# Attention's lead-in in a four-stage transformer kernel: queries of the first heads stacked in two halves, keys stacked ahead, GpSimd combining tiles 4 to 15 in batches of four gathers

## The chip, the cores and the metric

The kernel runs on one core of a Trainium2 chip, as one launch. The metric is the device time of that launch in microseconds (us), lower is better; the profile shows one execution of it. The engines are called as the profile calls them: PE (TensorE, matmuls), PEld (its weight loads), DVE (VectorE), ACT (ScalarE), POOL (GpSimd) and SP (SyncE). SPq, ACTq and POOLq are the instruction queues of those engines where they only wait or issue transfers.

## What is computed

The reference takes x of shape (4, 512, 512) and a context ctx of shape (4, 512, 128) through four steps, each added to x with a gate: a learned sparse adjacency, a mixture of 8 experts (two per token) with a shared expert, a grouped cross attention, and a feed-forward layer whose inputs are quantized in blocks of 32. The change touches the end of the second step and the beginning of the third:

```python
x = x + tanh(g_ffn[0]) * moe(layernorm(x))        # y = sum of two experts' rows, by weight; plus shared
# third step: q = layernorm(x) (4, 512, 512), k = v = ctx; 32 query heads, 8 key heads, head size 16
qh = q.reshape(B, S, 8, 4, 16).transpose(0, 2, 3, 1, 4)
kh = k.reshape(B, S, 8, 16).transpose(0, 2, 1, 3)
scores = einsum('bkgsd,bktd->bkgst', qh, kh) / 4
out = einsum('bkgst,bktd->bkgsd', softmax(scores), vh)
x = x + tanh(g_xattn[1]) * out
```

## The kernel before

All engine programs are written out by hand, each in its own order; semaphores tie them together, and nothing is reordered by a scheduler. The 2048 tokens are 16 tiles of 128 rows (TT = 16), four tiles to a batch (R = 4, B = 4). A tile of X is 128 x 512 in float32 and stays in SBUF.

The stages run one after the other: a (adjacency), b (experts), c (attention), d (feed-forward). At the end of stage b every token's two expert rows lie in a DRAM scratch. `gather(t)` (L1168) fetches both rows of tile t on POOL's queue with two indirect transfers of 256 KB, into one of four buffers `mgath`. Adding them to X by their weights is called combining here. DVE combines with `combine(t)` (L1726, L1731) and takes the tile's row statistics (L1736, bn_stats); POOL combines with `combine_late(t)`: two scalings (L1473), a sum (L1476) and an add to X (L1478). Before, DVE combines tiles 0 to 6 and POOL tiles 7 to 15 (`FIRST_LATE = 2 * R - 1`), where POOL issues the next tile's two gathers after each tile.

Attention works on groups: one group is one key head with its four query heads (G = 8 groups to a batch, HG = 4 heads). For each group PE first computes all scores once, with queries as rows, in eight slots (tp, h) of two 128 x 512 matmuls (L1629, `a_slot`), and DVE takes the row maxima of each slot from PSUM (L1798, `max_slot`). The maxima are transposed and laid into a row of QS, and PE computes the scores again with keys as rows (L1641, `b_slot`), ACT takes the exponentials (L1547) and PE multiplies them with V (L1652, `pv`). Maxima run two groups ahead: while group g goes through exponentials, the slots of group g + 2 are mixed in, and a slot's matmul waits until DVE is through with the slot two before it.

QS and KK hold queries and keys split into a high and a low float16 part and stacked in three terms, so each group needs three transfers of 64 KB for queries (`stack_queries`, or L1391 in `stack_group`) and three of 32 KB for keys. Before batch 0 there is a lead-in with the following steps: gathers of tiles 0 to 3; their combining and statistics on DVE; `moments(0, R)`, 4 aggregations and 12 small linked operations (L170 to L176) that give mean and reciprocal deviation; `norm(0, r)` (L1772); transposes on PE (L1604, `t_q`); the high part copied by ACT (L1520, `hi_q`), the low part by DVE (L1779, `lo_q`); the stacking of groups 0 and 1; 16 slots of scores and maxima for groups 0 and 1; then batch 0, group 0. ACT issues the keys of groups 0 and 1 (L1579), SP the queries (L1385). SP waits for the low part of the last row tile before it issues any:

```python
sp.wait_ge(t_free, tuse(None, "q", R - 1) + 1)
for g in range(2):
    stack_queries(0, g)
```

In DVE's batch 0, `combine_stats(t)` at places listed in STATS_AT takes the statistics of tiles that POOL combined (it waits on `mg_used`), and `moments_part` does the moments of tiles 4 to 7 in eight pieces during group 0 (L184 to L193: a seed of three operations, then squares and steps), which `norm(1, r)` needs from group 1 on. `values(0, h)` (L1465) fills V on POOL, eight small scalings behind two fills (L1456, L1460).

## Time and profile before

| | us |
|---|---|
| median of three runs | 1646.1 |
| lowest and highest run | 1642.47, 1647.3 |
| the profiled execution's own time | 1643.61 |
| its span, first to last instruction | 1641.7 |
| PE busy in the span | 1463.1 (89%) |
| DVE busy | 1208.8 (74%) |
| ACT busy | 745.2 (45%) |
| POOL busy | 555.6 (34%) |

Times in the rows are microseconds from the start of the span. The lead-in lies between the last expert matmul, which starts at 639.67, and batch 0 of attention at about 695; attention ends at about 1091. In rows of the timeline a group of equal instructions in a row is one line with its count, and its second number is from the first start to the last end. A matmul's duration holds its pipeline, so in a row of matmuls the distance between starts is what each costs. PEclk is the granted clock of TensorE: 1.00 is 2.4 GHz and 0.50 is 1.2 GHz.

### The profile page before, as it was taken

Reading aid. Unit: us, or ns where it says so; the run is one execution under the profiler, and the core shown is the slowest. Engines: PE = TensorE matmul, PEld = TensorE weight load, DVE = VectorE, ACT = ScalarE, POOL = GpSimd, SP = SyncE. Lnnn points to the kernel's source line nnn. Section 1 sums busy time; section 2 is a strip of 40 time slices with the busy share of each in tenths; the row PEclk is TensorE's granted clock in tenths of the full one; section 3 lists DMA queues with packets and bytes.
Section 4 is the critical chain, followed back from the end, with each engine's and each line's share of the span. In section 5 each row is a group of like instructions: output and inputs, shape, how many; then the busy total and the mean of one; then the engine's idle time right before and its main releaser. Section 6 shows DMA issues by size and latency. Waiting matters only on the chain.

```text
span 1641.7 us, 24188 instructions
## 1 busy us (share of the span) xinstructions
PE 1463.1 (89%) x8146; PEld 708.7 (43%) x8146; DVE 1208.8 (74%) x2087; ACT 745.2 (45%) x1346; POOL 555.6 (34%) x530
## 2 busy tenths in 40 slices
PE   3288898958999996599999999988999999999998
PEld 1145555635555563133232333324444454444444
DVE  6988889466999995999997988855555455555565
ACT  3664654224555555077777777761222222222212
POOL 2523334013676664871010000012323222322332
PEclk8589998988999998599999999999999999999999
DMA  4312222124556554672203011362000000000000
GB/s 158 106 52 68 67 73 86 48 78 152 191 179 191 183 181 130 159 141 48 44 2 59 7 27 32 52 114 41 1 0 26 0 0 15 11 0 0 26 13 13
DMA packets 114811, 113.79 MB, mean 69 GB/s; under 512 B 59416, under 2 KB 87320, under 8 KB 114720
## 3 DMA queue, kind: packets, MB, share of 16 engines
q1 hardware_dynamic: 106448, 89.64, 20.4%
q0 software_dynamic: 5680, 18.62, 4.1%
q10 hardware_dynamic: 2592, 4.39, 0.7%
q8 instruction: 49, 0.80, 0.2%
q14 instruction: 42, 0.34, 0.1%
HBM read 59.26 MB, written 31.20 MB: 55 GB/s over the span
## 4 chain that ended last, share of the span: by engine, by line
PE 61%; DVE 19%; POOL 6%; issue 6%; ACT 4%; DMA 3%; SPq 1%; DVEq 0%; POOLq 0%; ACTq 0%
PE PS L2213 18%; PE PS L2236 10%; PE PS L1039 7%; PE PS L1652 6%; PE PS L1641 6%; PE PS L1629 5%; PE PS L1054 3%; DVE WORK L1798 3%; POOL WORK L2054 2%; PE PS L2226 2%; POOL WORK L2061 1%; DMA WORK<-in_L_ffn_sw_dram 1%; DVE WORK L691 1%; ACT BIG L1547 1%; PE PS L1617 1%
## 5 line engine op out<-in xcount | busy, mean ns | idle before, releaser
L2213 PE MATMUL PS<-BIG 128*128 128x512 f16 x1536 | 337.9, 380 | 3.5 <-issue 2.1
L1798 DVE TENSOR_REDUCE WORK<-PS 128x2 f32<-128x1024 f32 x256 | 302.6, 1217 | 40.9 <-PE PS L1629 39.8
L1547 ACT ACTIVATE BIG<-PS 128x512 f32<-128x512 f32 x512 | 278.7, 596 | 91.6 <-PE PS L1641 86.2
L2213 PEld LDWEIGHTS PS<-BIG 128*128 128x128 f16 x1536 | 150.5, 98 | 182.2 <-issue 3.8
L1629 PE MATMUL PS<-BIG 128*128 128x512 f16 x512 | 189.5, 397 | 14.4 <-DMA BIG<-BIG 7.0
L1641 PE MATMUL PS<-BIG 128*128 128x512 f16 x512 | 193.6, 385 | 3.7 <-ACT BIG L1547 2.0
L1039 PE MATMUL PS<-BIG,WORK 128*128 (+1 forms) x1128 | 180.7, 318 | 14.8 <-DVE WORK L1074 8.0
L2236 PE MATMUL PS<-BIG 128*128 128x512 f16 x768 | 173.8, 379 | 1.8 <-DVE BIG L2308 1.8
L2139 ACT ACTIVATE WORK<-PS 128x512 f32<-128x512 f32 x64 | 38.1, 597 | 296.5 <-PE PS L2213 296.5
L2288 DVE SCALAR_TENSOR_TENSOR BIG<-PS,WORK 128x512 f32<-128x512 f32 x64 | 44.1, 690 | 136.9 <-ACT WORK L2139 136.8
L1039 PEld LDWEIGHTS PS<-BIG,WORK 128*128 128x128 f16 x1128 | 109.8, 99 | 79.2 <-issue 21.4
L1652 PE MATMUL PS<-BIG 128*32 128x512 f32 x1024 | 136.2, 604 | 0.6 <-ACT BIG L1547 0.6
L285 POOL TENSOR_TENSOR BIG<-WORK,BIG 128x704 f16<-128x704 f32 (+2 forms) x49 | 70.9, 1455 | 169.6 <-ACT BIG L269 169.5
L2004 POOL TENSOR_TENSOR BIG<-BIG,WORK 128x2048 f32<-128x2048 f32 (+1 forms) x19 | 59.9, 3153 | 194.5 <-DVE WORK L1993 194.5
L1641 PEld LDWEIGHTS PS<-BIG 128*128 128x128 f16 x512 | 48.9, 97 | 171.7 <-ACT BIG L1547 133.9
L2236 PEld LDWEIGHTS PS<-BIG 128*128 128x128 f16 x768 | 75.1, 98 | 81.8 <-DVE BIG L2308 2.0
L1054 PE MATMUL PS<-BIG,WORK 128*128 (+1 forms) x423 | 99.9, 382 | 5.6 <-DVE WORK L1083 4.7
L1039 PE MATMUL PS<-BIG 128*128 128x352 f16 x576 | 93.6, 321 | 1.5 <-DVE BIG L1074 1.5
L2008 POOL TENSOR_TENSOR BIG<-BIG,WORK 128x2048 f32<-128x2048 f32 (+1 forms) x19 | 59.2, 3115 | 66.8 <-DVE BIG L2000 66.8
L1629 PEld LDWEIGHTS PS<-BIG 128*128 128x128 f16 x512 | 49.7, 99 | 63.9 <-DVE WORK L1798 25.1
L2143 ACT ACTIVATE BIG<-PS 128x512 f16<-128x512 f32 x64 | 36.6, 596 | 84.4 <-PE PS L2226 84.4
L1465 POOL TENSOR_SCALAR BIG<-WORK,GATES 128x64 f32<-128x64 f32 x32 | 15.9, 502 | 172.1 <-PE PS L1652 171.9
(257 smaller groups left out, 2269.4 us busy)
## 6 DMA issues: line engine op xcount, KB each, us to landing
wdq_scratch<-WORK SPq DMA_DIRECT2D x48, 256.0 KB, 2.3
WORK<-in_L_ffn_w_dram SPq DMA_DIRECT2D x32, 352.0 KB, 3.5
y_scratch<-WORK SPq DMA_DIRECT2D x39, 256.0 KB, 2.1
BIG<-BIG SPq DMA_DIRECT2D x96, 64.0 KB, 2.3
X<-in_x_dram SPq DMA_DIRECT2D x4, 1024.0 KB, 9.0
WORK<-in_L_ffn_w_dram SPq DMA_DIRECT2D x16, 256.0 KB, 2.7
WORK<-in_L_ffn_gate_w_dram SPq DMA_DIRECT2D x16, 256.0 KB, 3.2
WORK<-in_L_ffn_up_w_dram SPq DMA_DIRECT2D x16, 256.0 KB, 3.3
```

What stands on the lines that cost most here:

```text
L285: nc.gpsimd.tensor_tensor(chunk_dst(j, slot, 1), chunk_stage(j), chunk_dst(j, slot, 0), ALU.subtract).then_inc(split_l, 1)
L1039: ins = nc.tensor.matmul(bank[1 + 2 * w13 + pair][:, 0:I], m.xT[:, p, a, k * P:(k + 1) * P], W13[:, bass.ds(slot * W13N + (w * half + k * ...
L1054: ins = nc.tensor.matmul(dst[:, :], m.hT[:, up, a, k * P:(k + 1) * P], W2[:, bass.ds(slot * W2N + (w * (W2N // 2) + k * D), D)], start=(fi ...
L1547: nc.scalar.activation(PB[:, tp, 2 * h + j, :], src, ACT.Exp, scale=SOFT_SCALE).then_inc(exp_ok, 1)
L1629: ins = nc.tensor.matmul(APAIR[h % 2][:, i, :], QS[:, g * HG + h, r * P:(r + 1) * P], KA[:, g, :], start=True, stop=True)
L1641: nc.tensor.matmul(BBANK_END[(2 * h + j) % 4] if end else BBANK[j], KS[:, g, t * P:(t + 1) * P], QS[:, g * HG + h, :], start=True, stop=Tr ...
L1652: ins = nc.tensor.matmul(OBANK[32 * h:32 * h + 32, :], V[:, t, g, :], PB[:, tp, 2 * h + j, :], start=(t == 0), stop=(t == R - 1))
L1798: v.tensor_reduce(MXU[:, g % 2, c:c + 2], APAIR[h % 2], AX_X, ALU.max, negate=True).then_inc(max_ok, 1)
L2004: nc.gpsimd.tensor_tensor(blocks(x), blocks(x), spread(sc[:, 1, :], nb), ALU.mult).then_inc(s.q_ok, 1)
L2008: nc.gpsimd.tensor_tensor(blocks(x), blocks(x), spread(sc[:, 2, :], nb), ALU.mult).then_inc(s.dq_ok, 1)
L2213: ins = nc.tensor.matmul(bank[b], fxT[:, p, a, k * P:(k + 1) * P], w[:, c, l, k, :], start=(i == 0), stop=(i == 3 * KD - 1))
L2236: ins = nc.tensor.matmul(dst, fhT[:, a, k, :], DW[:, k // KD, l, k % KD, :], start=(k == 0 and i == 0), stop=(k == FT - 1 and i == 2))
```

## The change

Five things change; what is computed and the instructions' shapes stay as they are, except that three query transfers become six.

- SP issues the queries of group 0 in two halves: the columns of row tiles 0 and 1 as soon as the low part of row tile 1 is there, the rest after row tile 3 with a semaphore of its own (`q_rest`), on which PE waits before the slots of tp = 1.
- ACT issues the keys of groups 0 and 1 before its copies `hi_q`, and DVE takes the keys' low part (`lo_ctx`) behind tile 0's combining instead of behind the moments.
- `FIRST_LATE = R`: DVE combines tiles 0 to 3 only, POOL tiles 4 to 15.
- POOL first fills KK's rows and V and runs `values(0, h)`, then works in three rounds: eight transfers that gather four tiles, then four tiles combined. Outputs of heads (`heads_in`) move to fit.
- The statistics of tiles 4 to 7 are taken by DVE in the first four slots of group 0 of batch 0, the pieces of their moments two to a slot in the last four slots; tiles 8 to 15 have theirs in groups 2 to 5 instead of 1 to 4.

```diff
@@ -1003,7 +1003,7 @@
         mg_in = [sem(f"mg_in{p}") for p in range(len(mgath))]
         mg_half = sem("mg_half")
         mg_used = sem("mg_used")
-        FIRST_LATE = 2 * R - 1
+        FIRST_LATE = R
 
         class Unit:
 
@@ -1334,6 +1334,7 @@
         t_hi = sem("t_hi")
         t_free = sem("t_free")
         qk_in = [sem(f"qk_in{g}") for g in range(G)]
+        q_rest = sem("q_rest")
         a_mm = sem("a_mm")
         max_ok = sem("max_ok")
         mt_ok = sem("mt_ok")
@@ -1379,10 +1380,11 @@
             def load_ctx(b):
                 sp.dma_start(CT, ctx_rows[:, bass.ds(b * R, R), :]).then_inc(ct_in, 16)
 
-            def stack_queries(b, g):
+            def stack_queries(g, cols, landed):
                 for n, (a, w) in enumerate(TERMS):
                     rows = slice(n * HD, (n + 1) * HD)
-                    sp.dma_start(QS[rows, g * HG:(g + 1) * HG, :], qhT[g * HD:(g + 1) * HD, a, :, :]).then_inc(qk_in[g], 16)
+                    sp.dma_start(QS[rows, g * HG:(g + 1) * HG, cols],
+                                 qhT[g * HD:(g + 1) * HD, a, :, cols]).then_inc(landed, 16)
 
             def stack_group(b, g):
 
@@ -1431,9 +1433,11 @@
             load_ctx(0)
             sp.wait_ge(pad_low, 1)
             sp.wait_ge(pad_high, 1)
+            sp.wait_ge(t_free, tuse(None, "q", 1) + 1)
+            stack_queries(0, slice(0, 2 * P), qk_in[0])
             sp.wait_ge(t_free, tuse(None, "q", R - 1) + 1)
-            for g in range(2):
-                stack_queries(0, g)
+            stack_queries(0, slice(2 * P, S), q_rest)
+            stack_queries(1, slice(0, S), qk_in[1])
             for g in range(2, 4):
                 stack_group(0, g)
             maxima(0, 0, 0)
@@ -1454,11 +1458,9 @@
         def c_gpsimd(pool):
             g = nc.gpsimd
             nc.gpsimd.memset(KK.rearrange("p a b c -> p (a b c)")[32:64, :].bitcast(F32), 0.0).then_inc(pad_low, 1)
-            for t in range(len(mgath), 2 * len(mgath)):
-                gather(pool, t)
             pool.wait_ge(pad_low, 1)
-            nc.gpsimd.memset(V.rearrange("p a b c -> p (a b c)"), 1.0).then_inc(v_ones, 1)
-            pool.wait_ge(v_ones, 1)
+            nc.gpsimd.memset(V.rearrange("p a b c -> p (a b c)"), 1.0).then_inc(pad_low, 1)
+            pool.wait_ge(pad_low, 2)
 
             def values(b, h):
                 nc.gpsimd.nop(nofuse=True)
@@ -1488,17 +1490,19 @@
             pool.wait_ge(ct_in, 16)
             for h in range(G):
                 values(0, h)
-            for t in range(R, TT - R):
-                if t >= FIRST_LATE:
+            for q in range(1, B):
+                for t in range(q * R, q * R + R):
+                    gather(pool, t)
+                if q == B - 1:
+                    heads_in(0, 1)
+                for t in range(q * R, q * R + R):
                     combine_late(t)
-                gather(pool, t + len(mgath))
+                if q == B - 2:
+                    heads_in(0, 0)
+            pool.wait_ge(ct_in, 32)
             for h in range(G):
-                if h < R:
-                    combine_late(TT - R + h)
-                if h > 0:
+                if h > 2:
                     heads_in(0, h - 1)
-                if h == 0:
-                    pool.wait_ge(ct_in, 32)
                 pool.wait_ge(pv_mm, (h + 1) * 2)
                 values(1, h)
             with pool.Fori(1, B - 1) as b:
@@ -1569,8 +1573,6 @@
             nc.scalar.nop().then_inc(exp_ok, 2)
             nc.scalar.nop().then_inc(o_sb, 1)
             hi_ctx(None)
-            for r in range(R):
-                hi_q(None, r)
             act.wait_ge(pad_low, 1)
             act.wait_ge(t_free, tuse(None, "q", 0))
             for g in range(2):
@@ -1578,6 +1580,8 @@
                     rows = slice(n * HD, (n + 1) * HD)
                     nc.scalar.dma_start(KK[rows, g, :, :], khT[g * HD:(g + 1) * HD, w, :].unsqueeze(1).to_broadcast([HD, 2, S])
                                         ).then_inc(qk_in[g], 16)
+            for r in range(R):
+                hi_q(None, r)
             maxima(None, -1, 0)
             batch(0, True, False)
             with act.Fori(1, B - 1) as b:
@@ -1705,6 +1709,8 @@
                 t_q(None, 0, r)
             for u in range(2):
                 for tp in range(2):
+                    if u == 0 and tp == 1:
+                        pe.wait_ge(q_rest, 16 * 3)
                     for h in range(HG):
                         a_slot(u, u, tp, h, lambda: pe.wait_ge(qk_in[u], 16 * 6), u > 0)
                 if u == 0:
@@ -1762,9 +1768,6 @@
                 else:
                     rsqrt_parts(link, MV[:, a:b, 1], RSTD[:, a:b], b - a)[i - 1]()
 
-            for t in range(R):
-                combine(t)
-            moments(0, R)
 
             def norm(b, r):
                 t = b * R + r
@@ -1838,9 +1841,10 @@
                             if ahead:
                                 max_slot(u + 2, g, tp, h)
                             if first and (g, tp, h) in STATS_AT:
-                                combine_stats(2 * R + STATS_AT.index((g, tp, h)))
-                            if first and g == 0:
-                                moments_part(R, 2 * R, tp * HG + h)
+                                combine_stats(R + STATS_AT.index((g, tp, h)))
+                            if first and g == 0 and tp == 1:
+                                moments_part(R, 2 * R, 2 * h)
+                                moments_part(R, 2 * R, 2 * h + 1)
                             if first and g == G - 1:
                                 moments_part(2 * R, TT, tp * HG + h)
                             if tp == 0 and h == 1 and not last and 1 <= g <= R:
@@ -1876,29 +1880,28 @@
                     rows_aggr(b)
                     rows_end(b)
 
+            combine(0)
+            lo_ctx(None)
+            for t in range(1, R):
+                combine(t)
+            moments(0, R)
             for r in range(2):
                 norm(0, r)
-            lo_ctx(None)
             for r in range(R):
                 if r < 2:
                     dve.wait_ge(t_mm, tuse(None, "q", r) + 1)
                     norm(0, r + 2)
                 lo_q(None, r)
-            for t in range(R, 2 * R - 1):
-                combine(t)
             for u in range(2):
                 for tp in range(2):
                     for h in range(HG):
                         max_slot(u, u, tp, h)
-                        if (u, tp, h) == (1, 1, 0):
-                            combine_stats(FIRST_LATE)
-            STATS_AT = [(g, *at) for g in range(1, 5) for at in ((0, 3), (1, 3))]
+            STATS_AT = [(0, 0, h) for h in range(R)] + [(g, *at) for g in range(2, 6) for at in ((0, 3), (1, 3))]
             batch(0, True, False)
             with dve.Fori(1, B - 1) as b:
                 batch(b, False, False)
             batch(B - 1, False, True)
 
-        v_ones = sem("v_ones")
         oo_ok = sem("oo_ok")
```

How the change moves the instructions, at three places. First DVE from the end of the lead-in's low parts through group 0 of batch 0, before (L1779 is the low part, L1726, L1731 and L1736 combine a tile and take its statistics, L1798 is a slot's maxima, L1747 and L184 to L193 are pieces of the moments):

```order
L1779 TENSOR_TENSOR BIG<-PS,BIG 128x4x128 x3
L1726 SCALAR_TENSOR_TENSOR X<-WORK,X 128x512
L1731 SCALAR_TENSOR_TENSOR X<-WORK,X 128x512
L1736 BN_STATS WORK<-X 128x6
...
L1798 TENSOR_REDUCE WORK<-PS 128x2 x13
L1736 BN_STATS WORK<-X 128x6
L1798 TENSOR_REDUCE WORK<-PS 128x2 x4
L1747 BN_AGGR MV<-WORK 128x2 x4
L1798 TENSOR_REDUCE WORK<-PS 128x2
L184 TENSOR_SCALAR NEWT<-MV 128x4
```

The same place after the change (lines are shifted by 3 to 6):

```order
L1782 TENSOR_TENSOR BIG<-PS,BIG 128x4x128 x3
L1801 TENSOR_REDUCE WORK<-PS 128x2 x17
L1742 BN_STATS WORK<-X 128x6
L1801 TENSOR_REDUCE WORK<-PS 128x2
L1742 BN_STATS WORK<-X 128x6
...
L1801 TENSOR_REDUCE WORK<-PS 128x2
L1753 BN_AGGR MV<-WORK 128x2 x4
L184 TENSOR_SCALAR NEWT<-MV 128x4
L185 TENSOR_SCALAR RSTD<-NEWT 128x4
L186 TENSOR_SCALAR NEWT<-NEWT 128x4
```

The three combined tiles ahead of the first maxima and the one set of statistics among the lead-in's 16 slots are gone; four sets of statistics stand behind the first four slots of group 0.

Second, POOL from the gathers of the lead-in on, before (L1168 is one gather transfer, L1456 and L1460 are the fills, L1465 the values, L1473 to L1478 combine a tile):

```order
L1168 DMA WORK<-y_scratch,WORK 128x512 x8
L1456 MEMSET BIG 32x4096
L1168 DMA WORK<-y_scratch,WORK 128x512 x8
L1460 MEMSET BIG 128x1024
L1465 TENSOR_SCALAR BIG<-WORK,GATES 128x4x16 x8
L1168 DMA WORK<-y_scratch,WORK 128x512 x6
L1473 TENSOR_SCALAR WORK<-WORK 128x512 x2
L1476 TENSOR_TENSOR WORK<-WORK 128x512
L1478 TENSOR_TENSOR X<-WORK,X 128x512
L1168 DMA WORK<-y_scratch,WORK 128x512 x2
```

and after:

```order
L1168 DMA WORK<-y_scratch,WORK 128x512 x8
L1460 MEMSET BIG 32x4096
L1462 MEMSET BIG 128x1024
L1467 TENSOR_SCALAR BIG<-WORK,GATES 128x4x16 x8
L1168 DMA WORK<-y_scratch,WORK 128x512 x8
L1475 TENSOR_SCALAR WORK<-WORK 128x512 x2
L1478 TENSOR_TENSOR WORK<-WORK 128x512
L1480 TENSOR_TENSOR X<-WORK,X 128x512
L1475 TENSOR_SCALAR WORK<-WORK 128x512 x2
```

The second eight gathers moved behind the fills and the values, and combining runs tile after tile with no gathers between.

Third, SP's queue at the stacking, before (L1380 loads the context, L1385 are queries of groups 0 and 1, L1391 and L1392 queries and keys of the groups after):

```order
L1380 DMA WORK<-in_ctx_dram 128x4x128
L1385 DMA BIG<-BIG 16x2048 x6
L1391 DMA BIG<-BIG 16x2048
L1392 DMA BIG<-BIG 16x2x512
L1391 DMA BIG<-BIG 16x2048
```

and after:

```order
L1381 DMA WORK<-in_ctx_dram 128x4x128
L1386 DMA BIG<-BIG 16x4x256 x6
L1386 DMA BIG<-BIG 16x2048 x3
L1393 DMA BIG<-BIG 16x2048
L1394 DMA BIG<-BIG 16x2x512
```

Group 0's three query transfers are six of half the size, of which three can go earlier; everything behind them on the queue follows three issues later.

## Rows read from the trace of the kernel before

**Rows 1.** The page, chain that ended last: shares of the span by engine.

```profile
PE 61%; DVE 19%; POOL 6%; issue 6%; ACT 4%; DMA 3%; SPq 1%; DVEq 0%; POOLq 0%; ACTq 0%
```

**Rows 2.** Windows: stretch, length, busy by PE, PEld, DVE, ACT, POOL, then PEclk, DMA, GB/s.

```profile
675.00:695.00 20.00, 15.79 (x33) 2.67 (x34) 18.45 (x18) 0.27 (x1) 17.08 (x19) 0.50 0.65 162
700.00:712.00 12.00, 9.84 (x55) 3.10 (x57) 11.59 (x21) 8.51 (x17) 10.52 (x12) 1.00 0.88 191
712.00:724.00 12.00, 12.00 (x74) 4.11 (x73) 11.81 (x15) 9.54 (x20) 11.01 (x12) 1.00 0.80 163
```

**Rows 3.** Chain in order of time: start, length, what, from the lead-in to group 0.

```profile
663.93 1.13 PE PS L1604 x4
...
668.70 0.70 DVE BIG L1779
...
669.49 0.64 SPq L1385
...
670.80 4.20 DMA BIG<-BIG
675.04 1.05 PE PS L1629 x2
676.11 9.43 DVE WORK L1798 x8
```

**Rows 4.** Timeline of DVE: start, length, line, operation, shapes, count, idle before.

```profile
666.77 1.39 DVE L1779 TENSOR_TENSOR BIG<-PS,BIG 128x512 f16<-128x512 f32 x2
...
672.25 0.75 DVE L1731 SCALAR_TENSOR_TENSOR X<-WORK,X 128x512 f32<-128x512 f32 x1
...
692.71 0.68 DVE L1736 BATCH_NORM_STATS2 WORK<-X 128x6 f32<-128x512 f32 x1
693.31 3.56 DVE L1798 TENSOR_REDUCE WORK<-PS 128x2 f32<-128x1024 f32 x3
697.35 1.23 DVE L1798 TENSOR_REDUCE WORK<-PS 128x2 f32<-128x1024 f32 x1 [0.48 <-PE PS L1629]
...
700.04 0.79 DVE L184 TENSOR_SCALAR NEWT<-MV 128x4 f32<-128x4 f32 x1
700.86 0.17 DVE L185 TENSOR_SCALAR RSTD<-NEWT 128x4 int32<-128x4 int32 x1
...
705.34 0.82 DVE L189 TENSOR_TENSOR NEWT<-RSTD 128x4 f32<-128x4 f32 x1
...
711.48 1.21 DVE L1798 TENSOR_REDUCE WORK<-PS 128x2 f32<-128x1024 f32 x1
```

**Rows 5.** Timeline of POOL, and ACT's one row of key transfers.

```profile
655.61 3.50 POOL L1456 MEMSET BIG<- 32x4096 f32 x1
...
670.71 5.22 POOL L1465 TENSOR_SCALAR BIG<-WORK,GATES 128x64 f32<-128x64 f32 x8 [0.21 <-POOL BIG L1460]
676.08 1.01 POOL L1168 DMA_INDIRECT WORK<-y_scratch,WORK  x1
...
683.40 1.36 POOL L1473 TENSOR_SCALAR WORK<-WORK 128x512 f32<-128x512 f32 x2
...
687.72 1.04 POOL L1168 DMA_INDIRECT WORK<-y_scratch,WORK  x1 [0.27 <-POOL X L1478]
...
699.53 1.27 POOL L1478 TENSOR_TENSOR X<-WORK,X 128x512 f32<-128x512 f32 x1
...
668.13 4.35 ACTq L1579 DMA_DIRECT2D BIG<-BIG  x6
```

**Rows 6.** Transfers issued in 694.5 to 698.5, then in 776 to 782: size, us to landing.

```profile
BIG<-BIG SPq DMA_DIRECT2D x4, 32.0 KB, 3.5
...
BIG<-BIG SPq DMA_DIRECT2D x5, 32.0 KB, 2.0
```

**Rows 7.** Windows as in Rows 2, in stage a, where the granted clock fell.

```profile
276.00:280.00 4.00, 1.90 (x27) 1.55 (x26) 3.97 (x4) 1.61 (x3) 4.00 (x3) 0.97 0.00 0
280.00:283.00 3.00, 3.00 (x11) 1.57 (x10) 2.82 (x7) 0.00 (x0) 2.76 (x3) 0.50 0.00 0
```

## The prediction

> **What bounds the kernel now.** I read the chain that ended last first: PE holds 61% of it and DVE 19% [rows 1]. That is an average, so the windows around the edit come next [rows 2]. From 675 to 695, the lead-in's 16 slots, DVE is busy 18.45 of 20.00 us and ACT 0.27: nothing goes through exponentials yet, and PE runs at a granted clock of 0.50, its lower level of 1.2 GHz. From 700 to 712, group 0 of batch 0, the clock is at 1.00, DVE is busy 11.59 of 12.00 and PE 9.84. From 712 on PE is busy 12.00 of 12.00 with DVE close behind at 11.81. So DVE sets the pace up to the end of group 0, and PE after it. A gain in the lead-in counts only if DVE does not lose it again in group 0.
>
> The chain in order of time gives the lead-in's path [rows 3]: the last low part ends at 669.40 (668.70 + 0.70), SP's first query issue starts at 669.49, the third transfer runs from 670.80 to 675.00, PE starts its slots at 675.04 and DVE its maxima at 676.11. Between 669.3 and 675.9 DVE combines tiles 4 to 6, in time that it would otherwise spend waiting for that transfer.
>
> **The lead: first queries earlier.** SP waits for row tile 1 instead of row tile 3. Two low parts in a row started at 666.77 and ended together at 668.16 [rows 4]; the first is row tile 1, so it ends about 0.69 after 666.77, at 667.46. With SP's lag from before (669.40 to 669.49) the first issue starts at 667.56, and the third, 1.31 behind it as 670.80 is behind 669.49 [rows 3], at 668.87. How long half a transfer takes beside a running gather has no row; the ends are 2.0 (32 KB with no gather) and 4.20 (64 KB among keys, queries and gathers), and the nearest is 3.5, 32 KB with gathers running [rows 3, 6]. I take 3.5, because in the changed order POOL's second eight gathers are in flight just then. Landing at 672.4 instead of 675.0: **2.6 earlier**, between 1.9 and 4.1.
>
> Edits that must hold for this and cost nothing: the keys. ACT can issue them once KK's fill is done at 659.11 [rows 5], and six issues took 4.35, so it is through at 663.5, while its first copy waits for transposes that end at 665.06 (663.93 + 1.13) [rows 3]. If that cover of 1.6 were gone, the difference would move the whole path. The keys' low part on DVE behind tile 0 is 0.69 of work at a place where DVE waits for gathers (tile 3's data come last either way). The second half of the queries is issued after 669.40 and behind three issues, so its third lands about where group 0's did before, at 675.0 or a little earlier; PE needs it after four slots, which take DVE 4.7 of the 9.43 for eight [rows 3], so at about 677. It is hidden by 2. What is queued behind it on SP (queries of group 1, then 12 issues and the maxima's row) has less lateness than the slots of groups 0 and 1 give it, 19 us from 676.11 to the end.
>
> Taking tiles 4 to 6 from DVE saves nothing by itself: they filled a wait. It has to be done, since their 6.6 us would now stand in front of the maxima. The statistics of tile 7 did stand among the slots, at 692.71, and the next slot started at 693.31 [rows 4]. **0.6 earlier.**
>
> **What comes back in group 0.** DVE takes the statistics of tiles 4 to 7 behind the first four slots of group 0, four times 0.60: **2.4 later**. Before, group 0 took DVE from 697.35 to 711.48, 14.13 without an idle row but for the 0.48 ahead of it [rows 4], so nothing there hides them, at either clock. The pieces of the moments are the same operations, only two to a slot. What they wait for on POOL may change. At 700.04 the first seed took 0.79, and its neighbour 0.17; POOL's add to X ran from 699.53 to 700.80 [rows 4, 5]. The 0.82 at 705.34 holds the same kind of excess, so the two largest make 0.62 + 0.65 = 1.3. DVE's small operations wait out a large POOL operation there.
>
> After the change POOL gets to its first round at about 665 (fill, V's fill, then eight values of 5.22 or less [rows 5]). Six gathers took 7.32, from 676.08 to 683.40; eight take about 9.8. A tile takes 4.05 (683.40 to 687.45, where POOL is free for the gather at 687.72 after 0.27). Tiles 4 to 7 are done at about 665 + 9.8 + 16.2 = 691, and DVE asks for the first at about 695: **no wait**. The second round gathers until about 701 and then combines without a pause up to 717. The moments' pieces come at about 702 to 709, so they meet POOL at work all the time, where before it was at work 4.05 of every 6.68. On the other side they stand in four bundles behind four slots rather than in seven. The bounds: all 1.3 gone, or each of four bundles waiting out two POOL operations of about 1.0 each (4.05 for four), 8 in all, 6.7 more. I take the value of before, **0 more**, as nearest row, with both ends kept.
>
> **POOL's values beside DVE's moments.** The eight values now run beside the lead-in's 12 linked operations and `norm`, which lie on the path. Before, they ran beside DVE's combining, and the combining operation at 672.25 took 0.75 as others did without POOL's company [rows 4]; POOL's eight took 5.22, so POOL waited rather than DVE. I take 0; the other end is 3.5, eight times a POOL operation of 0.44 if none could pass. The Trainium skill, SBUF — State Buffer, "Who interferes with whom", says that a DVE instruction with two SBUF inputs and a GpSimd instruction that reads SBUF exclude each other, and that the second to issue is held until the first is through. The 0.79 at 700.04 agrees with that; the 0.75 at 672.25 does not, as far as small POOL operations go. By the rule alone the sum would be up to 3.5 worse.
>
> **The sum.** -2.6 - 0.6 + 2.4 + 0 + 0 = -0.8 us. After group 0 PE is the bound and its work is unchanged; group 1 loses two sets of statistics and group 5 gains them, where DVE has room. The profiled execution took 1643.61, so it would take 1642.8; it lies 2.5 under the median of 1646.1, and I give the forecast against the median: 1645.3.
>
> **Rivals.** *The lead carries through.* The moments' pieces fall between POOL's operations and the half transfers land in 2.0: -4.1 - 0.6 + 2.4 - 1.3 = -3.6, 1642.5. For it: POOL's phase is free by several us. Against: gathers are in flight and combining is unbroken. *POOL holds up the moments.* Each of the four bundles loses 1.0 to 2.0 to POOL's combining: 4.0 to 8.0 instead of 1.3, so -0.8 + 2.7 to 6.7 = +1.9 to +5.9, 1648.0 to 1652.0: slower than before. It decides once the waits in group 0 exceed 1.3 + 0.8 = 2.1. For it: POOL without a pause from 701 to 717. *The values hold up the lead-in.* Up to +3.5, so +2.7, 1648.8; the row at 672.25 speaks against it, the skill's rule for it. *The clock.* In group 0 PE now has four matmuls for each 1.8 of DVE's work (3.56 for three slots, 1.19 each, and 0.60) in the first half. In stage a a stretch in which PE was busy 1.90 of 4.00 was followed by a granted clock of 0.50 [rows 7]; the 9.84 of 12.00 in group 0 before was not [rows 2]. A fall for three or four us makes the second half's matmuls twice as long and costs about 2: 1647.3. *The change does not do what it says*: the halves land after 4.2 beside the gathers, and 1.9 - 2.6 leaves -0.1: 1646.0, which the forecast's range holds.
>
> **How the numbers follow.** Forecast with its range of 1643.5 to 1647: 0.52. Lead carries through: 0.18. POOL holds up the moments: 0.18. Values: 0.05. Clock: 0.07. A measurement of this kernel can tell about 0.3% from no change, 4.9 us here. Faster by more than that needs the first rival with all its terms at their ends: 0.06. Slower by more needs the upper half of POOL's hold or two rivals at once: 0.05. The rest, 0.89, is within. The range of 8 in 10 reaches from 1641.0 to 1649.0: the forecast's terms between their bounds, the lower half of POOL's hold, and the runs' own spread, whose lowest lies 3.6 under their median.
>
> **What would show it.** In the changed profile: PE's first slot at about 672.4 instead of 675.04, with no wait on the second half before the fifth; DVE's maxima back to back from there; DVE's first maximum of group 0 at about 694.2 instead of 697.35, and group 1's first at about 710.7 instead of 711.48, so 3.2 gained and 2.4 lost again. Waits of DVE on POOL's tiles 4 to 7, key issues that end after 665, moments in the lead-in longer than before, or small operations in group 0 beyond 2.1 us of excess would each prove a step wrong. So would a span over 4.9 us shorter, since no term here is that large.

## The result and the profile after

The changed kernel takes 1647.83 us in the median of 20 runs, the kernel before 1644.31 in 20 runs beside them. The ratio is 1.0019, 95% interval 1.0010 to 1.0028: slower by 0.19%, some 3.1 us. One of the 20 runs of the changed kernel took 2214.41 at a mean granted clock of 0.647, against 0.947 to 0.953 in the other 19, and the ratio leaves it out. The change is smaller than the 0.3% that the prediction thought could be told, but the interval lies wholly above 1; the forecast was 0.8 us less. The 1647.83 is outside the forecast's own range (1643.5 to 1647) and inside the wide one (1641.0 to 1649.0). The forecast started from a median of 1646.1 for the kernel before; 3.1 more than that is 1649.2, just above the wide range. The profiled execution has a span of 1647.6.

The chain that ended last has the shares of before [rows 1], with PE at 60% instead of 61% and DMA at 2% instead of 3%:

```profile
PE 60%; DVE 19%; POOL 6%; issue 6%; ACT 4%; DMA 2%; SPq 1%; DVEq 0%; POOLq 0%; ACTq 0%
```

So the windows come next, as in [rows 2]: stretch, length, busy by PE, PEld, DVE, ACT and POOL, then the granted clock, DMA share and GB/s. The three stretches are the lead-in's 16 slots, group 0 of batch 0, and the start of group 1:

```profile
676.00:696.00 20.00, 16.33 (x35) 2.77 (x34) 17.92 (x16) 0.27 (x1) 18.56 (x20) 0.50 0.51 111
700.00:717.00 17.00, 11.13 (x59) 3.25 (x57) 16.55 (x28) 8.91 (x17) 15.79 (x18) 1.00 0.73 167
717.00:724.00 7.00, 5.89 (x37) 2.04 (x36) 6.62 (x7) 4.80 (x10) 1.84 (x2) 1.00 0.10 18
```

Group 0 is where the change shows. PE was busy 9.84 of 12.00 there [rows 2] and is now busy 11.13 of 17.00; DVE is busy nearly throughout, and POOL 15.79 of 17.00.

The lead did come earlier. The chain in order of time, as in [rows 3] (start, length, what), from the low part of row tile 1 to the first maxima:

```profile
669.87 0.61 DVE BIG L1782
...
670.57 0.76 SPq L1386
...
672.01 3.56 DMA BIG<-BIG
...
675.62 1.05 PE PS L1633 x2
676.69 3.59 DVE WORK L1801 x3
```

Its times can't be set beside those of before directly, because this execution reached the end of stage b later: the last row of expert matmuls starts at 642.27, against 639.67. All times in the next table are worked out as the start of a row minus the start of that last expert row in the same trace. "Excess" is what the 12 small operations of the moments in group 0 (L184 to L193) took in all beyond 0.165 us each, which is about what one takes with POOL idle.

| us after the last expert row | before | after |
|---|---|---|
| PE's first slot | 35.38 | 33.35 |
| DVE's first maximum | 36.45 | 34.42 |
| group 0's first maximum | 57.68 | 55.14 |
| group 1's first maximum | 71.82 | 74.61 |
| length of group 0 | 14.13 | 19.47 |
| group 2's first maximum | 84.13 | 86.59 |
| batch 1's first maximum | 159.19 | 162.02 |
| end of the span | 1002.03 | 1005.30 |
| excess of the 12 small operations | 1.59 | 4.60 |

The changed kernel is 2.5 us ahead at the start of group 0 and 2.8 behind at its end. The whole loss arises in group 0, and it is still there at batch 1 (2.8) and at the end (3.3). DVE's timeline there (start, length, line, operation, shapes, count, idle before) shows what group 0 is made of now; [rows 4] are the rows of before:

```profile
663.82 0.20 DVE L170 TENSOR_SCALAR NEWT<-MV 128x4 f32<-128x4 f32 x1
...
676.69 9.48 DVE L1801 TENSOR_REDUCE WORK<-PS 128x2 f32<-128x1024 f32 x8 [4.29 <-PE PS L1633]
687.50 9.42 DVE L1801 TENSOR_REDUCE WORK<-PS 128x2 f32<-128x1024 f32 x8 [1.33 <-PE PS L1633]
697.41 1.23 DVE L1801 TENSOR_REDUCE WORK<-PS 128x2 f32<-128x1024 f32 x1 [0.49 <-PE PS L1633]
698.55 0.69 DVE L1742 BATCH_NORM_STATS2 WORK<-X 128x6 f32<-128x512 f32 x1
...
705.85 1.01 DVE L184 TENSOR_SCALAR NEWT<-MV 128x4 f32<-128x4 f32 x1
706.90 0.63 DVE L185 TENSOR_SCALAR RSTD<-NEWT 128x4 int32<-128x4 int32 x1
707.57 0.63 DVE L186 TENSOR_SCALAR NEWT<-NEWT 128x4 f32<-128x4 f32 x1
708.23 1.23 DVE L1801 TENSOR_REDUCE WORK<-PS 128x2 f32<-128x1024 f32 x1
709.37 0.16 DVE L189 TENSOR_TENSOR NEWT<-RSTD 128x4 f32<-128x4 f32 x1
709.57 0.16 DVE L190 TENSOR_TENSOR NEWT<-NEWT 128x4 f32<-128x4 f32 x1
709.77 1.13 DVE L193 SCALAR_TENSOR_TENSOR RSTD<-NEWT,RSTD 128x4 f32<-128x4 f32 x1
...
712.45 1.12 DVE L193 SCALAR_TENSOR_TENSOR RSTD<-NEWT,RSTD 128x4 f32<-128x4 f32 x1
...
714.95 0.62 DVE L190 TENSOR_TENSOR NEWT<-NEWT 128x4 f32<-128x4 f32 x1
715.60 0.63 DVE L193 SCALAR_TENSOR_TENSOR RSTD<-NEWT,RSTD 128x4 f32<-128x4 f32 x1
```

Beside it POOL's timeline, where [rows 5] stood before:

```profile
663.25 3.35 POOL L1467 TENSOR_SCALAR BIG<-WORK,GATES 128x64 f32<-128x64 f32 x8 [0.21 <-POOL BIG L1462]
...
691.45 1.26 POOL L1480 TENSOR_TENSOR X<-WORK,X 128x512 f32<-128x512 f32 x1
692.87 1.04 POOL L1168 DMA_INDIRECT WORK<-y_scratch,WORK  x1 [0.15 <-POOL X L1480]
...
705.57 1.26 POOL L1480 TENSOR_TENSOR X<-WORK,X 128x512 f32<-128x512 f32 x1
706.82 1.35 POOL L1475 TENSOR_SCALAR WORK<-WORK 128x512 f32<-128x512 f32 x2
708.26 1.26 POOL L1478 TENSOR_TENSOR WORK<-WORK 128x512 f32<-128x512 f32 x1
709.60 1.28 POOL L1480 TENSOR_TENSOR X<-WORK,X 128x512 f32<-128x512 f32 x1
```

The two views are read together by ends. The seed at 705.85 ends at 706.86, POOL's add at 706.83. The next two operations, 0.63 each, end at 707.53 and 708.20, POOL's pair of scalings (706.82, 1.35) at 708.17. The step at 709.77 ends at 710.90, POOL's add at 710.88. Each long small operation ends within 0.03 of the end of a POOL operation; it is called held below. There are 7 of these in group 0, against 3 before: the 0.79 and 0.82 of [rows 4] and this one:

```profile
710.38 0.46 DVE L193 SCALAR_TENSOR_TENSOR RSTD<-NEWT,RSTD 128x4 f32<-128x4 f32 x1
```

The rows also show why unbroken combining costs more than its share of time. Before, the seed was held once, until POOL's add ended at 700.80. POOL then went over to a gather, so the next operation, at 700.86, took 0.17 [rows 4]:

```profile
701.07 1.05 POOL L1168 DMA_INDIRECT WORK<-y_scratch,WORK  x1 [0.27 <-POOL X L1478]
```

Now the end of one POOL operation is the start of the next, so the following small operation is held again. And being held sets DVE's phase. Released at 708.20, DVE runs a maximum and the first operation of a square, which ends at 709.53, just as POOL's next operation does (708.26 + 1.26). One operation of 0.16 slips in, POOL's add starts at 709.60, and the step at 709.77 waits out nearly the whole of it. Then the same happens again (1.12 at 712.45).

### The profile page after: what moved, and what is told of

It reads as the page before. It is cut to its first block, busy times and chain, and to the rows that moved or that the text cites. A ratio compares the mean times of both kernels' runs of the same rounds, so it can differ in the third digit from the quotient of the medians.

```text
span 1647.6 us, 24194 instructions
## 1 busy us (share of the span) xinstructions
PE 1465.8 (89%) x8146; PEld 709.9 (43%) x8146; DVE 1208.3 (73%) x2081; ACT 744.9 (45%) x1346; POOL 565.4 (34%) x542
## 4 chain that ended last, share of the span: by engine, by line
PE 60%; DVE 19%; POOL 6%; issue 6%; ACT 4%; DMA 2%; SPq 1%; DVEq 0%; POOLq 0%; ACTq 0%
PE PS L2216 18%; PE PS L2239 10%; PE PS L1039 7%; PE PS L1656 6%; PE PS L1645 6%; PE PS L1633 5%; PE PS L1054 4%; DVE WORK L1801 3%; POOL WORK L2057 2%; PE PS L2229 2%; POOL WORK L2064 1%; DMA WORK<-in_L_ffn_sw_dram 1%; DVE WORK L691 1%; ACT BIG L1551 1%; PE PS L1621 1%
## 5 line engine op out<-in xcount | busy, mean ns | idle before, releaser
L1487 POOL TENSOR_TENSOR X<-WORK,X 128x256 f32<-128x256 f32 (+1 forms) x32 | 23.2, 726 | 157.1 <-DVE WORK L1812 157.1
```

## The experiments

All ratios are to the kernel before, run on the same chip. The theory is that of the rival in the prediction: POOL's combining holds up the moments' small operations.

**POOL pauses while the moments run.** The changed kernel with one wait in POOL's loop, ahead of the combining of tiles 8 to 11:

```diff
+                if q == B - 2:
+                    pool.wait_ge(qn_ok, R + 1)
                 for t in range(q * R, q * R + R):
                     combine_late(t)
```

> The changed kernel with one wait added: GpSimd gathers tiles 8 to 11 as it did, but combines them only after VectorE has normalized tile 4 for batch 1, so that no combining runs beside the moments' pieces of group 0. Theory 1 (the pieces wait out GpSimd's combining): the excess of the twelve small operations over 0.17 each falls from 4.6 us to under 0.5, group 0 gets 4 to 4.6 us shorter, and the kernel comes out 1.4 us under the kernel before (ratio 0.9991) instead of 3.2 over it. Rival A (VectorE's own work in group 0 is the loss: four sets of statistics, pieces in bundles of two): group 0 keeps its length within 1 us and the ratio stays at about 1.002.

Measured: ratio 0.999, interval 0.9977 to 1.0002. DVE's and POOL's timelines in that kernel:

```profile
704.46 0.17 DVE L184 TENSOR_SCALAR NEWT<-MV 128x4 f32<-128x4 f32 x1
...
706.59 0.16 DVE L193 SCALAR_TENSOR_TENSOR RSTD<-NEWT,RSTD 128x4 f32<-128x4 f32 x1
```

```profile
713.78 1.36 POOL L1475 TENSOR_SCALAR WORK<-WORK 128x512 f32<-128x512 f32 x2 [11.36 <-DVE WORK L1777]
```

With POOL waiting 11.36, the seed takes 0.17 instead of 1.01 and the step 0.16 instead of 1.13. The excess falls from 4.60 to -0.03, group 0 from 19.47 to 14.85: 4.62 less, the whole excess and no more. The ratio falls by 0.0029, 4.8 us, and the two intervals do not overlap. The cause of the loss is shown by this run: the operations, their number and their order on DVE are those of the changed kernel, only POOL is still. Against the kernel before, it is not shown to be faster: the interval reaches over 1.

**Combining and gathers alternate again.** The changed kernel, but POOL issues the gathers of one tile after each combined tile, as before:

```diff
-            for q in range(1, B):
-                for t in range(q * R, q * R + R):
-                    gather(pool, t)
...
-                for t in range(q * R, q * R + R):
-                    combine_late(t)
+            for t in range(R, 2 * R):
+                gather(pool, t)
+            for t in range(R, TT):
+                combine_late(t)
+                if t + R < TT:
+                    gather(pool, t + R)
...
```

> The changed kernel with GpSimd's batches undone from tile 4 on: one tile combined, then the two gathers of the tile four further on, as in the kernel before. Theory 1: GpSimd combines 4.05 of every 6.7 us while the pieces run, so about six tenths of the 4.6 us of waits are left, 2.8; the kernel is 1.4 us over the kernel before (1.0008). Rival A: no change against the changed kernel, 1.002. Rival C (the combining of tiles 4 to 7 then ends too late for the statistics): VectorE waits before the fourth set of statistics, whose tile is combined at about 701, and the time is over 1.002.

Measured: 1.0007, interval 0.9995 to 1.0019. The excess is 2.45 and group 0 takes 17.31, so 2.15 and 2.16 less than in the changed kernel. DVE and POOL:

```profile
702.40 1.17 DVE L185 TENSOR_SCALAR RSTD<-NEWT 128x4 int32<-128x4 int32 x1
703.61 0.17 DVE L186 TENSOR_SCALAR NEWT<-NEWT 128x4 f32<-128x4 f32 x1
```

```profile
702.29 1.27 POOL L1480 TENSOR_TENSOR X<-WORK,X 128x512 f32<-128x512 f32 x1
703.83 1.04 POOL L1168 DMA_INDIRECT WORK<-y_scratch,WORK  x1 [0.27 <-POOL X L1480]
```

A single hold can be as long as ever (1.17, within 0.03 of POOL's end), but the gather behind it lets the next operation through in 0.17. Of the 3.0 by which the excess had grown, 2.15 thus goes with the batching of gathers. The other 0.86 (2.45 against 1.59) may go with the order of the pieces and POOL's phase; no run tells these apart.

**The lead alone.** The kernel before with the half transfers, the earlier keys and the earlier `lo_ctx`; DVE still combines tiles 4 to 6 and POOL's order is that of before:

```diff
...
+            sp.wait_ge(t_free, tuse(None, "q", 1) + 1)
+            stack_queries(0, slice(0, 2 * P), qk_in[0])
             sp.wait_ge(t_free, tuse(None, "q", R - 1) + 1)
-            for g in range(2):
-                stack_queries(0, g)
+            stack_queries(0, slice(2 * P, S), q_rest)
+            stack_queries(1, slice(0, S), qk_in[1])
...
```

> The kernel before with the first part of the change alone: queries of group 0 in two halves, keys stacked ahead of ScalarE's copies, the keys' low part behind tile 0. VectorE still combines tiles 4 to 6 before the first maxima and GpSimd keeps its order. Theory 1: TensorE's first slot starts 2 to 3 us earlier, VectorE's first maximum less than 0.5 us earlier because it is busy combining until then, and the time is that of the kernel before within 0.5 us (ratio 1.000). Rival D (an earlier lead is worth its length whatever VectorE does): 2.6 us faster, 0.9984.

Measured: 1.0003, interval 0.9989 to 1.0017. PE's first slot comes at 33.61, 1.77 earlier than before, DVE's first maximum at 36.32, 0.13 earlier. DVE's timeline says why:

```profile
676.59 0.69 DVE L1742 BATCH_NORM_STATS2 WORK<-X 128x6 f32<-128x512 f32 x1
677.20 9.47 DVE L1800 TENSOR_REDUCE WORK<-PS 128x2 f32<-128x1024 f32 x8
```

The statistics of tile 6 run right up to the maxima, with no idle time between. The three tiles that filled the wait of before now stand in the way, so the earlier transfer is worth nothing unless some of them leave DVE. The excess is 1.87 here, with the pieces and POOL's order of before, so a shift of phase alone moved it by 0.28.

**Whole queries.** The changed kernel with its queries in whole transfers after row tile 3:

```diff
-            sp.wait_ge(t_free, tuse(None, "q", 1) + 1)
-            stack_queries(0, slice(0, 2 * P), qk_in[0])
             sp.wait_ge(t_free, tuse(None, "q", R - 1) + 1)
-            stack_queries(0, slice(2 * P, S), q_rest)
+            stack_queries(0, slice(0, S), qk_in[0])
...
```

> The changed kernel with the halves undone: SyncE waits for row tile 3 and issues whole queries for groups 0 and 1; all else as changed. Theory 1: the lead of 2.0 us (first slot against the last expert matmul) is lost and nothing else changes, so the kernel is 2 us slower than the changed one, 5.2 over the kernel before (1.0032). Rival B (the halves gain nothing because gathers hold them up): same as the changed kernel, 1.002.

Measured: 1.003, interval 1.0016 to 1.0044. PE's first slot comes at 35.61, 2.26 later than in the changed kernel; batch 1 begins 1.55 later (163.57 against 162.02), and the ratio is 0.0011 higher, 1.8 us. The two ratios' intervals overlap, so the times alone do not show it; the trace's 1.55 speaks for the same size. By that pair of traces the halves keep most of what they gain at the first slot, as long as DVE has nothing in front of its maxima. The excess in group 0 is 4.12, near that of the changed kernel, as it should be.

**Short statistics.** The changed kernel with the statistics of tiles 4 to 7 over 32 columns instead of 512:

```diff
-                v.bn_stats(bnst_c[:, t, :], X[:, t, :]).then_inc(row_st, 1)
+                v.bn_stats(bnst_c[:, t, :], X[:, t, 0:32] if R <= t < 2 * R else X[:, t, :]).then_inc(row_st, 1)
```

> The changed kernel with the statistics of tiles 4 to 7 taken over the first 32 columns of a row instead of 512, so the moments of these tiles are those of 32 columns and the output is not the reference's. It prices the term of 2.4 us. If that term is right (four sets of 0.60 each lie open in group 0), the first four slots of group 0 get 4 x 0.5 = 2.0 us shorter (0.69 against about 0.18 for a short one), and group 0 with them, give or take the waits on GpSimd, which change phase. If TensorE at its lower clock hid them, group 0 gets less than 1 us shorter.

Measured: 1.0005, interval 0.9994 to 1.0015; group 0 takes 17.21, 2.26 less, of which 0.29 is a smaller excess (4.31). One statistics operation:

```profile
694.32 0.18 DVE L1742 BATCH_NORM_STATS2 WORK<-X 128x6 f32<-128x32 f32 x1
```

About 0.5 saved four times is what group 0 loses in length: in group 0 of this kernel each microsecond on DVE is a microsecond of the path, for the statistics as for the holds.

**Half operations on POOL.** The changed kernel with POOL's operations on tiles 8 to 11 split into two of 256 columns each:

```diff
+                parts = [slice(0, D // 2), slice(D // 2, D)] if 2 * R <= t < 3 * R else [slice(0, D)]
...
-                g.tensor_tensor(m[:, 0, :], m[:, 0, :], m[:, 1, :], ALU.add).then_inc(mg_half, 1)
+                for n, c in enumerate(parts):
+                    ins = g.tensor_tensor(m[:, 0, c], m[:, 0, c], m[:, 1, c], ALU.add)
+                ins.then_inc(mg_half, 1)
...
```

> The changed kernel, no pause, with GpSimd's operations on tiles 8 to 11 cut into halves of 256 columns. Theory 1 with the length of one GpSimd operation as the price: each wait of a small operation lasts at most 0.75 us (a half sum) instead of 1.13, and the excess of the twelve falls from 4.6 us, to 2.3 if their number stays; since halves follow each other without a semaphore between, more of the twelve may have to wait, so up to 4.6. If a wait lasted for GpSimd's whole row of queued operations, single excesses would stay at 1 us or more.

One execution, 1647.87, too little to rank by time. The trace tells the size of a hold:

```profile
703.37 0.73 DVE L184 TENSOR_SCALAR NEWT<-MV 128x4 f32<-128x4 f32 x1
704.14 0.65 DVE L185 TENSOR_SCALAR RSTD<-NEWT 128x4 int32<-128x4 int32 x1
...
706.82 0.58 DVE L193 SCALAR_TENSOR_TENSOR RSTD<-NEWT,RSTD 128x4 f32<-128x4 f32 x1
```

The longest falls from 1.13 to 0.73, the excess from 4.60 to 3.04. A hold gets shorter with the POOL operation beside it (two half sums now take 1.41); there are 8 holds instead of 7, and the sum falls by a third and not by half.

**Pause, and tile 4 back on DVE.** The changed kernel with the pause, and with one tile combined by DVE in its wait for the queries, which also takes one statistics operation out of group 0:

```diff
-        FIRST_LATE = R
+        FIRST_LATE = R + 1
...
+                if q == B - 2:
+                    pool.wait_ge(qn_ok, R + 1)
-                for t in range(q * R, q * R + R):
+                for t in range(max(q * R, FIRST_LATE), q * R + R):
...
+            for t in range(R, FIRST_LATE):
+                combine(t)
...
```

> The kernel with GpSimd's pause, and tile 4 given back to VectorE, which combines it in its wait for the first scores and takes its statistics there, so that group 0 holds three sets of statistics. Expected by theory 1: the first slot and the first maximum stay where they are, group 0 is 0.6 us shorter than with the pause alone (14.2 instead of 14.85), and the time is 2.0 us under the kernel before (0.9988). Rival: GpSimd's first tile now waits for VectorE's and the statistics of tile 7 come late, so nothing is gained.

Measured: 0.9981, interval 0.9969 to 0.9993: faster than both kernels, 3.1 us under the kernel before. In DVE's timeline the tile fits into the wait with 2.44 left over:

```profile
672.31 0.69 DVE L1746 BATCH_NORM_STATS2 WORK<-X 128x6 f32<-128x512 f32 x1
675.44 9.49 DVE L1805 TENSOR_REDUCE WORK<-PS 128x2 f32<-128x1024 f32 x8 [2.44 <-PE PS L1637]
```

Group 0 takes 14.23 with an excess of -0.04, and batch 1 begins at 157.03, 2.16 earlier than before. That tile 4 on DVE adds anything to the pause is not shown by the times: the intervals overlap (the changed kernel with the pause has 0.9977 to 1.0002), and in that run's trace batch 1 began at 156.77, after a lead-in whose 16 slots ran 1.2 faster, in part at a granted clock of 1.00.

**Pause, and tiles 4 and 5 back on DVE.** The same with `FIRST_LATE = R + 2`.

> As with tile 4, and tile 5 too goes back to VectorE ahead of the first maxima. Its gathers landed at 674.6 in the changed kernel, and a tile takes VectorE 2.2 us with its statistics, so it is done at 676.8 against a first maximum at 676.69. Expected: the first maximum 0 to 0.3 us later, group 0 another 0.6 shorter (13.6), the time 2.3 us under the kernel before (0.9986). Rival: the two tiles hold up the first maxima by more than they save, and the time is that of the version with tile 4 or above.

Measured: 0.9983, interval 0.9971 to 0.9994, not to be told from the last. The wait is now used up; the maxima follow the statistics without a gap:

```profile
675.29 0.69 DVE L1746 BATCH_NORM_STATS2 WORK<-X 128x6 f32<-128x512 f32 x1
675.90 9.47 DVE L1805 TENSOR_REDUCE WORK<-PS 128x2 f32<-128x1024 f32 x8
```

Group 0 takes 13.88, so 0.35 less than with tile 4 alone where 0.6 was expected, and batch 1 begins at 156.84.

**The pause alone, in the kernel before.**

```diff
+                if t == FIRST_LATE + 2:
+                    pool.wait_ge(qn_ok, R + 1)
                 if t >= FIRST_LATE:
                     combine_late(t)
                 gather(pool, t + len(mgath))
+            heads_in(0, 0)
...
```

> The kernel before with the pause alone: POOL waits for the first norm of group 1 before it combines tile 9, so nothing large runs on POOL beside the moments' twelve small operations in group 0 (before: tiles 9 and 10). The output of head 0 moves up two places on POOL to fit. Theory (the small operations lose time to POOL's combining, in the kernel before as well): their excess goes from 1.59 us to about 0, group 0 becomes 1.6 shorter, and the whole is 1.6 us faster, ratio 0.999; the earlier lead and the pause are then separate gains that add up to what the kernel with tile 4 on DVE showed (0.9981, 3.4 us faster). Rival (that kernel's gain is the pause alone): ratio 0.998, no difference to it. Rival (POOL's later tiles and values hold up attention afterwards, which cancels it): 1.000 or above, with group 0 shorter and the time lost in groups 1 to 5.

Measured: 0.9996, interval 0.9986 to 1.0005. The excess goes from 1.59 to -0.08 and group 0 from 14.13 to 12.67, so the kernel before had the same loss in a smaller size. The 1.6 us are seen in group 0; in the time they are not shown, since the interval reaches over 1. In DVE's and POOL's timelines:

```profile
702.69 0.16 DVE L184 TENSOR_SCALAR NEWT<-MV 128x4 f32<-128x4 f32 x1
```

```profile
715.57 1.36 POOL L1473 TENSOR_SCALAR WORK<-WORK 128x512 f32<-128x512 f32 x2 [16.35 <-DVE WORK L1775]
```

Of the 1.44 that group 1 begins earlier, 0.69 is left at batch 1; the rest goes in the groups between, which no run took apart. The rival that the pause alone explains the 0.9981 is not borne out: 0.9981 is outside this interval. It is not excluded either, since the two intervals overlap between 0.9986 and 0.9993. That the gains of the lead and of the pause simply add up is not borne out by the medians (alone they gave 1.0003 and 0.9996), but intervals this wide cannot exclude it. What the runs show is that the lead moves DVE's first maximum by only 0.13 while tiles 4 to 6 stay on DVE, and that tiles on POOL without the pause make the kernel slower.

**All runs together.** In the seven traces where POOL combines beside the moments' pieces 36 small operations are held, and each ends 0.01 to 0.05 after a POOL operation. Group 0 less its excess takes 14.86 to 14.88 in the five runs with the changed kernel's work on DVE (changed, pause, alternating, whole queries, half operations) and 12.54 to 12.74 in the three with the work of before (before, lead alone, before with the pause). So besides the statistics the holds account for the length of group 0 to within 0.2.

## Why the prediction was wrong

Each step, in the prediction's order, with what the changed profile shows. Times are from the table above.

| step | predicted | measured |
|---|---|---|
| lead, first slot of PE | -2.6 (-1.9 to -4.1) | -2.03 |
| tile 7's statistics out of the lead's slots | -0.6 | -0.5 |
| four statistics in group 0 | +2.4 | +2.3 (group 0 less its excess: 14.87 against 12.54); 2.0 of it gone in the run with short ones |
| waits on POOL's combining in group 0 | 0 more (-1.3 to +6.7) | +3.0 |
| values beside the lead-in's moments | 0 (up to +3.5) | 0.1; 0.6 in three later runs |
| group 1's first maximum | -0.8 | +2.8 |

**The step that failed is the term "0 more" for what the moments' pieces wait for on POOL.** It measured 4.60 against 1.59, 3.0 more. The prediction had seen the cause: it names POOL's unbroken combining from 701 to 717 (measured: 702.78 to 718.92) and has a rival for just this, from 1.9 to 5.9 slower, which decides once the waits exceed 2.1. It then took the excess of before as the nearest row and gave the rival 0.18. That row was not near, and it was read at 1.3, the two largest holds, where the 12 operations had 1.59. Before, POOL combined 4.05 of every 6.68, and behind the hold of the seed came a gather, so the next operation took 0.17 [rows 4]. After, there is no gather to slip through, and every bundle has three linked operations. Scaling the excess of before by POOL's busy share alone (6.68 over 4.05, so 1.65 times 1.59) would have given 2.6, already 1.0 more and past the 2.1 from which that rival decides. Of the rest the seed has a large part: its three operations, held one behind the other, have an excess of 1.78 (0.68 before). The run with a still POOL takes the 4.6 away, and the one with alternating gathers takes half of it away. So the forecast falls, and the rival "POOL holds up the moments" is what happened, in the lower half of its range: 4.6 in its four bundles, where it had 4.0 to 8.0.

**The lead** was 0.6 smaller than predicted, still within its bounds. Most of that lies ahead of the transfer: the data of tile 3 land later (DVE combines it from 661.10, 18.83 after the last expert row; before 18.53), so the moments of the lead-in start 21.55 after that row instead of 21.24, and with a slightly slower chain of small operations the low part of row tile 1 ends 0.41 later. SP's third issue comes 1.44 behind its first instead of 1.31. The transfer itself took 3.56, where 3.5 was taken from [rows 6]; the changed kernel's row for these three transfers, as in [rows 6], has a median of

```profile
BIG<-BIG SPq DMA_DIRECT2D x3, 32.0 KB, 3.4
```

so the choice among 2.0, 3.5 and 4.20 was right.

**The covers held.** The keys are issued at 662.06 and through 3.96 later, ahead of ACT's first copy at 668.09:

```profile
662.06 3.96 ACTq L1581 DMA_DIRECT2D BIG<-BIG  x6
```

Their end at 666.02 is past the 665 that the prediction named as a sign of error, but only because this execution runs later as a whole: it is 23.75 after the last expert row, where the predicted 663.5 is 23.83 after the row of before.

PE waited 4.58 for the first half of the queries and nowhere for the second. DVE did not wait for POOL's tiles: tile 7 is combined at 692.71 (691.45 + 1.26), and the first statistics run at 698.55; the prediction said 691 and 695. The eight values on POOL (663.25 to 666.60) ran beside the lead-in's moments, whose 12 operations took 0.16 to 0.20 each, 0.20 for the first one shown above. In the runs with whole queries, with short statistics and with tile 4 on DVE one of them took 0.51, and the 12 had an excess of about 0.6. The value 0 for this term stands within that, and its rival (+3.5) did not happen.

The two sides of the Trainium skill's rule (SBUF — State Buffer, "Who interferes with whom": a DVE instruction that needs the port it shares with GpSimd and a GpSimd instruction exclude each other, and the second to issue is held until the first is through) come apart here. For POOL's operations of 128 x 512 the trace agrees, with holds of up to 1.13 beside operations of 1.27, ending together. For those of 128 x 64 (3.35 for eight, 0.42 each) the same small operations show next to nothing: 0.1 to 0.6 for the 12, where the prediction worked out up to 3.5 by the rule. In the kernel before, where the same eight ran beside DVE's combining, they took 5.22 [rows 5] and DVE's combining 0.73 to 0.77 an operation, about the 0.75 of elsewhere: there POOL was the one that waited. Whether it is the size of the operations that decides was not tried.

**The clock** was no cause. From 700 to 717 the granted clock stayed at 1.00, though PE was busy only 11.13 of 17.00, so the rival that it would fall did not happen. It did fall in group 0 in two other runs, the ones with whole queries and with half operations (windows as above):

```profile
710.80:714.20 3.40, 3.21 (x12) 1.50 (x16) 3.23 (x8) 1.03 (x2) 3.24 (x5) 0.50 0.89 190
```

```profile
706.60:710.00 3.40, 3.40 (x12) 1.45 (x16) 3.24 (x6) 1.28 (x3) 3.26 (x6) 0.50 1.04 222
```

Their group 0 less its excess took 14.86 and 14.87, as in the changed kernel (14.87). So the 2 us that the prediction put on such a fall were not there.

The terms as measured, -2.0 - 0.5 + 2.3 + 3.0, make +2.8, and the trace has +2.8 at group 1. What is behind it adds little: group 1 gets 0.3 back for its two sets of statistics (11.98 instead of 12.31), and batch 1 begins 2.8 behind. The prediction's belief that nothing after group 0 hides or adds much was right for this change. The end of the span is 3.3 behind, near the 3.1 of the ratio, but that closeness is in part luck: ends of single executions vary more, and that of the kernel before with the pause is 2.2 behind the kernel before, at a ratio of 0.9996.

## What to carry to other kernels

Here a chain of 12 short, linked VectorE operations lost 4.60 us beside a GpSimd that combined without a pause, 2.45 where gathers stood between, and nothing beside a still GpSimd. A link of 0.165 could wait for most of a GpSimd operation of 1.27, and the next link for the one after it. So before moving work to GpSimd, look for such chains in the same stretch, count links and not only busy shares, and try keeping GpSimd still while the chain runs (here with one wait). An earlier transfer counted only once the engine that uses its data had less filler work in front of it. How much filler to leave there is open: of the two versions faster than the kernel before, one left 2.44 of the wait unused and the other nothing, and they cannot be told apart.

## What the runs showed of the hardware

Not only the operations with two SBUF inputs were held. The seed, L184 to L186, are operations with one tile as input and constants, and took 1.01, 0.63 and 0.63. The prediction was wrong to read the 0.79 of before, also L184, as a case of the rule on two SBUF inputs. The statistics (0.69 at 698.55, and 0.69 at 703.72 with POOL combining) and the maxima from PSUM (1.21 to 1.23 throughout) were not. The Trainium skill (SBUF — State Buffer, "Who interferes with whom") names `tensor_scalar` among the operations that can take the shared port, if their operands meet its conditions, and says that `tensor_reduce` never does on trn2; these rows agree with both. Which property of an operation decides was not tried.

The granted clock rose once in the lead-in of the changed kernel, and fell again. Windows of that kernel:

```profile
667.00:671.00 4.00, 3.89 (x16) 2.94 (x16) 3.15 (x6) 1.79 (x3) 3.08 (x4) 0.50 0.44 125
671.00:674.40 3.40, 0.04 (x1) 0.00 (x0) 0.86 (x2) 0.60 (x1) 2.48 (x4) 1.00 0.83 213
674.40:698.00 23.60, 18.71 (x39) 3.49 (x40) 19.43 (x17) 1.46 (x3) 21.24 (x22) 0.50 0.57 132
```

PE had been transposing from 667 to 671 when its clock went from 1.2 to 2.4 GHz, idled for the queries at 2.4 GHz, and did the 16 slots at 1.2 GHz. In the first run with a pause the clock also stood at 1.00 from 684.7 to 688.1 and from 691.5 on, and group 0's first maximum came 1.1 earlier than in the changed kernel (54.04 against 55.14). The 16 slots themselves took 19.53 there, from DVE's first maximum to group 0's, against 20.72. So between these two executions the clock in the lead-in is worth about 1 us, which bounds what a single profile can tell.
